# Row loads of the expert loop moved from SyncE to ScalarE, and VectorE's third gate product set ahead of the way in

## The reference, cut to what matters

```
xn = layernorm(x)
x  = x + attention(xn, w_qkv, w_out, decay) + ffn(xn)

# ffn
logits = xn @ router_w.T
gate   = sigmoid(max(logits));  e = argmax(logits)
xs     = xn * gate
routed = (silu(xs @ Wg[e]) * (xs @ Wu[e])) @ Wd[e]      # 256 -> 2*512 -> 256
shared = (silu(xn @ Sg) * (xn @ Su)) @ Sd
ffn    = routed + shared
```

## Time and profile before

| | |
|---|---|
| median of 3 runs | 125.23 us (125.21 to 125.71) |
| the profiled execution's own time | 124.46 us |
| its span in the trace | 122.8 us |
| TensorE busy with matmuls | 116.4 us (95%) |
| VectorE busy | 83.8 us (68%) |
| ScalarE busy | 47.2 us (38%) |
| GpSimd busy | 44.9 us (37%) |
| mean data rate of the DMA engines | 205 GB/s |
| granted TensorE clock | full in all slices |

### The profile page before, as it was taken

The page is one execution under the profiler, slowest core; times in us unless marked ns, Lnnn a source line. Parts: engine busy times, 40 slices in busy tenths (PEclk is TensorE's granted clock), DMA queues, the critical chain, the costliest instruction groups (busy, mean ns, idle before and its releaser), DMA issues.

```text
span 122.8 us, 2394 instructions
## 1 busy us (share of the span) xinstructions
PE 116.4 (95%) x757; PEld 100.6 (82%) x757; DVE 83.8 (68%) x186; ACT 47.2 (38%) x93; POOL 44.9 (37%) x80
## 2 busy tenths in 40 slices
PE   4989999999999999997999899999899999999991
PEld 1257876788888875997999899999799988999990
DVE  0789678999969996929692939696623456933382
ACT  0667799917987845420303030323030308100000
POOL 7904040018688800000617070704360600887300
PEclk9999999999999999999999999999999999999999
DMA  3692799999999525861799999999941322233254
GB/s 94 179 323 31 284 331 238 165 166 187 404 398 390 213 61 83 334 189 37 193 358 314 339 243 355 285 351 310 324 111 44 68 57 52 59 91 112 85 185 156
DMA packets 21069, 25.18 MB, mean 205 GB/s; under 512 B 9081, under 2 KB 18817, under 8 KB 20033
## 3 DMA queue, kind: packets, MB, share of 16 engines
q1 hardware_dynamic: 18128, 20.91, 58.9%
q0 software_dynamic: 1664, 3.25, 8.3%
q10 hardware_dynamic: 1264, 0.88, 2.3%
HBM read 18.95 MB, written 6.08 MB: 204 GB/s over the span
## 4 chain that ended last, share of the span: by engine, by line
PE 40%; DMA 38%; POOL 6%; SPq 6%; issue 4%; DVE 3%; POOLq 0%; ACTq 0%; DVEq 0%
DMA sorted_rows<-zeros 17%; PE ps L1141 16%; DMA wqkv<-sorted_rows 13%; PE ps L1150 7%; POOL sorted_rows L471 6%; PE ps L313 6%; PE ps L315 6%; PE ps L314 5%; SPq L364 4%; DMA wqkv<-in_L_attn_w_qkv_dram 4%; DMA x_sb<-in_L_attn_x_dram 2%; DVE xgT L823 2%; DMA sorted_rows<-xn,slot_row 2%; SPq L330 1%; DVE wqkv L851 1%
## 5 line engine op out<-in xcount | busy, mean ns | idle before, releaser
L324 POOL DMA_DIRECT2D sorted_rows<-yrow x28 | 16.1, 579 | 38.2 <-DVE yrow L846 37.9
L1141 PE MATMUL ps<-xgT,gu 128*128 128x144 f32 x192 | 24.5, 286 | 0.0
L1141 PEld LDWEIGHTS ps<-xgT,gu 128*128 128x128 f32 x192 | 24.0, 190 | 0.1
L605 ACT ACTIVATE rz<-ps 128x144 f32<-128x144 f32 (+1 forms) x24 | 7.9, 330 | 36.4 <-PE ps L1141 36.4
L851 DVE TENSOR_TENSOR wqkv<-rz,ps 128x144 f32<-128x144 f32 (+1 forms) x24 | 8.1, 340 | 8.9 <-ACT rz L605 8.8
L1150 PE MATMUL ps<-wqkv,dn 128*128 128x144 f32 x96 | 13.0, 288 | 0.7 <-DVE wqkv L851 0.7
L1150 PEld LDWEIGHTS ps<-wqkv,dn 128*128 128x128 f32 x96 | 12.3, 197 | 1.0 <-DVE wqkv L851 1.0
L313 PE MATMUL ps<-xT_hi,sgu_hi 128*128 128x512 f32 x32 | 12.9, 402 | 0.0
L315 PE MATMUL ps<-xT_hi,sgu_lo 128*128 128x512 f32 x32 | 12.7, 396 | 0.0
L314 PE MATMUL ps<-xT_lo,sgu_hi 128*128 128x512 f32 x32 | 12.7, 396 | 0.0
L494 POOL DMA_INDIRECT q_sb<-sorted_rows,done_row x8 | 8.4, 1048 | 8.8 <-DMA sorted_rows<-yrow 6.7
(11 more groups left out here) (166 smaller groups left out, 228.7 us busy)
## 6 DMA issues: line engine op xcount, KB each, us to landing
gu<-in_L_ffn_w_gate_up_dram SPq DMA_DIRECT2D x6, 1024.0 KB, 6.6
dn<-in_L_ffn_w_down_dram SPq DMA_DIRECT2D x6, 512.0 KB, 8.2
sorted_rows<-zeros SPq DMA_DIRECT2D x1, 2608.0 KB, 20.4
xT_raw<-in_L_ffn_w_gate_up_dram SPq DMA_DIRECT2D x2, 1024.0 KB, 5.2
wqkv<-sorted_rows SPq DMA_DIRECT2D x40, 40.0 KB, 2.9
sorted_rows<-yrow POOLq DMA_DIRECT2D x28, 40.0 KB, 5.1
sgu<-_ffn_shared_gate_up_dram SPq DMA_DIRECT2D x1, 1024.0 KB, 6.1
ez<-in_L_ffn_w_down_dram SPq DMA_DIRECT2D x2, 512.0 KB, 6.8
```

The source lines that it names most:

```text
L324: eng.dma_start(rows.rearrange("(j p) f -> p j f", p=SQ), yrow[q * SQ:(q + 1) * SQ, b, :, :]).then_inc(s_store, 16)
L605: A(silu_part(h), ps[:, GATE[h], 0:len(PARTS[h]) * SLOTS], ACT.Silu).then_inc(s_silu, 1)
L1141: ins = mm(ps[:, (GATE, UP)[u][h], j * SLOTS:(j + 1) * SLOTS], gu_of[p][:, kc, col:col + P], xgT[:, kc, 0:SLOTS], start=(kc == 0), stop=(k ...
```

## The change

ScalarE issues the row loads of the loop, behind its third SiLU of each tile. SyncE keeps the first row load (tile 0), and the weights. VectorE does its third gate product ahead of `sorted_in`. In ScalarE's program tiles 0 to 6 are written out, so the loads' addresses are constants there; only the loop over the tiles from 7 on has them in registers.

```
+        def sorted_load(eng, first, s_load):
+
+            for q in range(P // SQ):
+                rows = sorted_rows[bass.ds(first, NSQ * SQ), q * SQ * KC:(q + 1) * SQ * KC]
+                eng.dma_start(xg[q * SQ:(q + 1) * SQ, :, :], rows.rearrange("(j p) f -> p j f", p=SQ)).then_inc(s_load, 16)

 # SyncE
-            def rows_of(e):
-
+            def refill(e):
+
+                p = e % 3
                 ends.append(sp.value_load(plan[0:1, e:e + 1], min_val=e + 1, max_val=TILES))
-                with sp.Fori(ends[e - 1] if e else 0, ends[e]) as t:
-                    sp.wait_ge(s_xgc, t + 2)
-                    sorted_load(t * SLOTS + 3 * SLOTS, s_xg)
-
-            def refill(e):
-
-                p = e % 3
-                rows_of(e)
                 done = ends[e]
                 sp.wait_ge(s_gup, 3 * done)
                 sp.dma_start(gu_of[p][:, :, :], gu_dram[e + 3]).then_inc(s_gu[p], 16)
...
-            sorted_load(SLOTS, s_xg0)
+            sorted_load(sp, SLOTS, s_xg0)
...
             sp.wait_ge(s_plan, 1)
-            sp.wait_ge(s_xgc, 1)
-            sorted_load(2 * SLOTS, s_xg)
             for e in range(E - 3):
                 refill(e)
-            for e in range(E - 3, E):
-                rows_of(e)
+            total = sp.value_load(plan[0:1, E - 1:E], min_val=E, max_val=TILES)
             sp.wait_ge(s_lastrow, 1)
...
 # ScalarE
                 for h in range(3):
                     act.wait_ge(s_gup, 3 * t + (h + 1))
                     A(silu_part(h), ps[:, GATE[h], 0:len(PARTS[h]) * SLOTS], ACT.Silu).then_inc(s_silu, 1)
-
+                act.wait_ge(s_xgc, t + 2)
+                sorted_load(act, t * SLOTS + 3 * SLOTS, s_xg)
+
+            act.wait_ge(s_xgc, 1)
+            sorted_load(act, 2 * SLOTS, s_xg)
             hidden_hi(LAST - 1)
             expert_tile(0)
...
 # VectorE
             def expert_tile(t):
                 expert_part(t, 0)
                 expert_part(t, 1)
+                expert_part(t, 2)
                 dve.wait_ge(s_xg, 64 * t + 64)
                 dve.wait_ge(s_gup, 3 * t + 3)
                 sorted_in()
-                expert_part(t, 2)
```

More of the change, by code:

```diff
@@ L359, in _ @@
             ends = []
[L361 to L364, removed]
-            def rows_of(e):
-                ends.append(sp.value_load(plan[0:1, e:e + 1], min_val=e + 1, max_val=TILES))
-                with sp.Fori(ends[e - 1] if e else 0, ends[e]) as t:
-                    sp.wait_ge(s_xgc, t + 2)
-                    sorted_load(t * SLOTS + 3 * SLOTS, s_xg)
             def refill(e):
                 p = e % 3
-                rows_of(e)
+                ends.append(sp.value_load(plan[0:1, e:e + 1], min_val=e + 1, max_val=TILES))
                 done = ends[e]
@@ L392, in _ @@
             sp.wait_ge(s_plan, 1)
-            sp.wait_ge(s_xgc, 1)
-            sorted_load(2 * SLOTS, s_xg)
             for e in range(E - 3):
                 refill(e)
-            for e in range(E - 3, E):
-                rows_of(e)
+            total = sp.value_load(plan[0:1, E - 1:E], min_val=E, max_val=TILES)
             sp.wait_ge(s_lastrow, 1)
             for q in range(2):
-                row_store(sp, ends[7], 1, q, s_ylast_sp)
-            sp.wait_ge(s_xg, 64 * ends[7] + 64)
+                row_store(sp, total, 1, q, s_ylast_sp)
+            sp.wait_ge(s_xg, 64 * total + 64)
             for i in range(1, NT, 2):
```

## The result

The changed kernel takes **127.70 us** (median of 4 executions, 127.44 to 127.96); the kernel before, measured with it, 125.22. The ratio is 1.021 with a 95% interval of 1.014 to 1.028: slower, clear of noise. The forecast was 125.7, in a range of 122.9 to 127.4, with 0.39 on slower.

A forecast was written before the change was run, and what follows sets the result against it. The loop was taken as bound partly by TensorE, partly by late rows, losing 2.50 us. With R = 7.9, S(6) came 0.44 us later than 87.60, giving 124.9 profiled and 125.7 on the median; range 122.9 to 127.4.

The forecast's parts named there:

- R: Time from the 1 MB weight load's issue to the last row piece's landing; taken as 7.9 us, bounds 7.3 and 8.4.
- What the rows' landing becomes: Part sizing the landing of ScalarE's row loads beside weights from GpSimd's stores: 7.9 us, called the unknown.
- the sum: Expert loop: S(t+2) is the later of S(t+1) + 5.88 and S(t) + 4.2 + R + 0.62.
- S(0): Start of tile 0 on TensorE's timeline, S(t) being that of tile t; the forecast used 49.82.
- The stores by which R was sized: GpSimd's 40 KB stores in their own queue beside weights: five sets landed 7.5 to 8.4 us after the 1 MB issue.
- The subtraction: Sizing of R: 0.2 us off the stores' mean of 8.1, since an undisturbed row piece lands that much sooner.
- rival 1: Rows overtake the weights, R below 7.06, all 2.50 us return: 122.8; sign: landing under 4 us beside weights; chance 0.30.
- VectorE's work behind tile 4: If rows bind, tile 5's first product comes 5.22 us behind the way in's start, stalling TensorE's down product 0.7 us.
- Rival 3: ScalarE becomes late: row issues of 0.9 us each would delay the first SiLU 1.3 us; 126.6; chance 0.05.
- The product order: VectorE's third product ahead of the way in: late rows forgiven 0.74 us, next load released about 0.4 us later.
- Rival 2: Rows sink behind the weights because SyncE refills earlier, at S(t) + 4.2; with R = 9.0, 128.9; chance 0.20.
- case one: The likeliest case, with R = 7.9: 125.7 us, its own range 124.1 to 127.2; chance 0.42.

The follow-up runs named there:

- the set of 8.6 us: A row set in the changed kernel with each 0.5 MB refill cut to a 32 KB piece; that run's two executions took 125.59 and 123.0 us.

## Why the prediction was wrong

**The step that failed** is the size of R in "What the rows' landing becomes": "I take R = 7.9", with 8.4 as the upper bound. The four row sets that were waited for behind a refill of the loop show 7.5, 9.8, 7.6 and 9.2, mean 8.5. In the second measurement of the changed kernel there are five: 8.5, 9.1, 8.5, 7.9 and 8.9, mean 8.6. The rule of the sum held. With the measured R's and S(0) = 50.38 it gives S(6) = 90.78, against 90.70 in the trace; with the forecast's S(0) = 49.82 it gives 90.22, on the median 127.85, against 127.70 measured. So the mis-sized term explains the miss by itself.

Two things in the sum hid it. It took one R three times, as if every late set were alike. In the trace S(6) hangs on two late sets only, those of 9.8 (tile 3) and 9.2 (tile 6), with undisturbed tiles 1 and 4 between. And the forecast had the volume and the rate at hand and did not divide one by the other: at TensorE's pace 1.9 MB a tile leaves the DMA engines no slack.

**What makes R larger** is only in part known. It is no constant, and it is larger where refills follow closely. In the changed kernel, twice measured, and in the run with the new queue and the old product order, four sets came behind a refill 5.9 to 6.2 us after the one before it: 9.0 to 9.8. Ten came behind one 6.5 us or more after: 7.1 to 9.2, mean 8.2. That fits a backlog that is built up and worked off, but it does not show it, for the weights held until the rows are in gave 9.3 once without a backlog. In the set of 9.8 a part can be seen: 34 of its 640 packets started from 68.0 to 69.4 us, beside the next 1 MB, issued at 66.87. This next refill stands there because it now comes at S + 4.2.

**The stores by which R was sized** were no stand-in. Four of their five refills came 5.6 to 6.7 us behind another and still gave 7.5 to 8.3 us; the rows came ahead of those refills in the same queue.

**The subtraction** of 0.2 us, from mean 8.1 to 7.9, went in the wrong direction and alone cost 0.6 in the sum. The rows show 0.1 as well, 1.9 less 1.8 us. A further slip changed no number of the sum: R at which TensorE binds is 11.76 - 4.82 = 6.94 us, and not the 7.06 of rival 1, which one expectation repeats.

**What was right.**
- The chain: S(t+1) = landing + 0.62. From landings 0.03 before the ways in of 62.08, 70.25, 82.66 and 90.13 it gives 62.67, 70.84, 83.25 and 90.72; measured 62.65, 70.81, 83.22 and 90.70.
- The 1 MB load at S + 4.2: 60.47 - 56.36 = 4.11, 66.87 - 62.65 = 4.22.
- The rows finish with the whole 1.5 MB in the changed kernel: the last landed at 70.22, the 0.5 MB issued at 62.43 took 7.3 us, to 69.7.
- VectorE's work behind tile 4 stalls the down product of tile 5: it was forecast 5.22 us behind the start of the way in and started 87.93 - 82.66 = 5.27 behind it, with TensorE idle for 0.52. This cost nothing here, since tile 6 then waited 0.54 us more for its rows.
- ScalarE's issues: 2.0 us for four forecast, 1.8 measured, and the SiLU behind them kept its time (64.91 - 62.65 = 2.26). One set took 2.95 us (at 96.01), and the SiLU behind it came 0.3 us late without effect. Rival 3 falls.
- Behind the loop nothing became late: from S(7) to the end of the span are 29.3 us in both kernels.

```profile
62.63 1.79 ACTq L330 DMA_DIRECT2D wqkv<-sorted_rows  x4
64.91 0.41 ACT L596 ACTIVATE rz<-ps 128x288 f32<-128x288 f32 x1 [4.14 <-PE ps L1136]
...
96.01 2.95 ACTq L330 DMA_DIRECT2D wqkv<-sorted_rows  x4
99.16 0.41 ACT L596 ACTIVATE rz<-ps 128x288 f32<-128x288 f32 x1 [3.94 <-PE ps L1136]
```

**The product order** was taken to forgive 0.74 us for each late set. Measured alone it gives 0.2 and 0.3%, with zero in both intervals. The 0.4 us by which the next load is released later, which the forecast called free "Where weights are what the rows wait for", and tile 4's work may take the rest; no run separates them.

**Rival 1** (rows overtake) does not hold in the changed kernel. One set landed in 3.1 to 3.4 us beside weights, under the 4 us named as a sign of it. But it was issued late, from 70.79 us on, and its last piece was in about 8.5 us behind the 1 MB load's issue. The sets that were waited for landed within 0.6 us of the last of the weights, which is at odds with any turn that favours small pieces. By the Trainium skill (DMA: Bandwidth & Descriptors, "Arbitration" under "Queues, rings and completion order") the engines take turns between queues, a packet from each. The last 11 row packets of the run with the rows asked for first agree: they started mostly 0.32 us apart, while 8 KB packets of weights of 0.31 us each ran.

**Rival 2** had the mechanism that the experiments bear out, the earlier refill. Its price of 128.9 was 1.2 us above the measured 127.70, case one's 125.7 was 2.0 below.

The sentence of the Trainium skill (same page, "Issuing engines are not separate DMA queues") that a second issuer saves only issuing time leaves open whether it can do harm. With the rows asked for first, the second queue gave 1.015 (1.000 to 1.029) where one queue gave 0.998 (0.992 to 1.004): likely harm, not shown by these executions.

## What to carry to other kernels

Before transfers are reordered or spread over queues, divide the bytes of a period by the measured rate: where that is as long as the period, a transfer on the critical path that is issued behind bulk lands when the bulk has landed, in a queue of its own as well, and bulk that is asked for earlier than needed only gets in its way. Here a second small buffer, which lets the critical load be asked for a period earlier, was worth more than any order of issue that was tried. A spread of some per cent between executions that shrinks when the bulk is taken away, or when the critical load gets slack, points to the same place. And a forecast that takes one landing time for every period should ask how far the landing times scatter, for the late ones are what the loop waits for.

## What was not expected of the hardware

- The spread: 122.3 to 126.0 us for the same kernel before, 0.26 us over ten executions once rows had slack.
- GpSimd's stores landed sooner in the changed kernel: median 2.2 us, 5.1 before. It is not the rows' queue that does it. With ScalarE issuing the rows and the refills behind them the median is 4.8, and in one queue with the weights first 3.8. It goes with the time of the refills; nothing was run on it.
- A DMA issue on ScalarE's queue or SyncE's mostly takes 0.32 to 0.46 us, but a few take 1.0 to 1.7 (at most 1.66 us in the changed kernel, 1.44 before). Their cause is open.
- A row set could land 8.4 us behind the issue of a 1 MB load that was itself in after 5.5. Its last 40 packets of 640 were behind the rest, as in the set of 8.6 us: one sixteenth of a transfer can hold the whole.
